# Adjacency columns shared by groups of four edge tiles with half-precision cells, and a reordered set-up

## The reference, cut to what matters

```python
# layer 0
m = silu(einsum('ei,ej,ijh->eh', x[dst], edge_attr_8, W_msg_tp) / sqrt(128))
agg = segment_sum(m @ W_msg_lin / 4, src)
# layer 1, six times, with different W
h = x @ W
agg = segment_sum(h[src] * norm[:, None], dst)      # norm = dinv[src] * dinv[dst]
h = leaky(agg + h * dinv**2 + b)
```

## Time and profile before

| | us |
|---|---|
| median of 3 runs (11523.59 to 11538.84) | 11527.22 |
| profiled execution, its time | 11525.68 |
| its span, first to last instruction | 11523.9 |
| PE busy in the span | 8973.8 |
| DVE busy | 7298.7 |
| POOL busy | 6700.9 |
| ACT busy | 4035.9 |

### The profile page before, as it was taken

The page is one execution under the profiler, slowest core; times in us unless marked ns, Lnnn a source line. Parts: engine busy times, 40 slices in busy tenths (PEclk is TensorE's granted clock), DMA queues, the critical chain, the costliest instruction groups (busy, mean ns, idle before and its releaser), DMA issues.

```text
span 11523.9 us, 201355 instructions
## 1 busy us (share of the span) xinstructions
PE 8973.8 (78%) x51270; PEld 6020.0 (52%) x51270; DVE 7298.7 (63%) x14361; ACT 4035.9 (35%) x11725; POOL 6700.9 (58%) x6789
## 2 busy tenths in 40 slices
PE   0499999998488998857666666688888868888886
PEld 0266666663367777742222222455555645555554
DVE  1498999995122222227777777677777767777776
ACT  2445333332000010005555555344444434444443
POOL 0588788777100000007777777577777757777775
PEclk9999999996588888855555555555555555555555
DMA  6733443440887877882222222111111111111111
GB/s 240 249 98 101 119 109 108 108 109 5 290 282 250 269 245 247 296 279 37 39 38 38 38 38 38 25 20 20 20 20 20 20 21 20 20 20 20 20 20 20
DMA packets 1340632, 1146.59 MB, mean 99 GB/s; under 512 B 329039, under 2 KB 1225504, under 8 KB 1340190
## 3 DMA queue, kind: packets, MB, share of 16 engines
q1 hardware_dynamic: 1108690, 1064.47, 29.1%
q0 software_dynamic: 210560, 44.35, 5.2%
q10 hardware_dynamic: 21186, 34.95, 1.2%
HBM read 994.01 MB, written 144.62 MB: 99 GB/s over the span
## 4 chain that ended last, share of the span: by engine, by line
POOL 31%; PE 14%; issue 12%; DMA 8%; DVE 7%; DVEq 1%; ACT 1%; SPq 1%; POOLq 0%; ACTq 0%
POOL arena L569 31%; PE ps L820 8%; DMA arena<-adj 5%; DVE msg L1779 3%; PE ps L754 2%; DVE arena L1774 2%; DMA arena<-tab,idx 2%; PE ps L935 2%; DVE acc L1266 1%; PE ps L797 1%; PE ps L633 1%; ACT x_all L1106 0%; SPq L455 0%; DMA arena<-rT 0%; DVE x_all L1606 0%
## 5 line engine op out<-in xcount | busy, mean ns | idle before, releaser
L569 POOL DMA_INDIRECT arena<-tab,idx x4896 | 4675.6, 955 | 3843.8 <-DMA idx<-in_src_p 2290.4
L935 PE MATMUL ps<-w_w2b,arena 33*128 33x256 f32 x6528 | 2928.1, 639 | 603.1 <-DMA arena<-rT 594.9
L935 PEld LDWEIGHTS ps<-w_w2b,arena 33*128 33x128 f32 x6528 | 2103.8, 330 | 1223.1 <-issue 686.9
L598 POOL DMA_INDIRECT adj<-pairs x1632 | 1868.7, 1145 | 491.4 <-issue 420.8
L1266 DVE TENSOR_TENSOR acc<-acc,ps 48x128 f32 x4920 | 1377.7, 280 | 660.0 <-DVE acc L1266 12.6
L820 PE MATMUL ps<-arena 128*128 128x192 bf16 (+1 forms) x18816 | 1341.5, 234 | 229.9 <-DMA arena<-adj 214.4
L820 PEld LDWEIGHTS ps<-arena 128*128 128x128 bf16 x18816 | 1282.7, 103 | 303.0 <-issue 293.7
L1774 DVE TENSOR_TENSOR arena<-ps,arena 128x512 f32<-128x512 f32 x1632 | 1012.8, 682 | 190.2 <-DMA arena<-tab,idx 186.6
L633 PEld LDWEIGHTS ps<-arena,threes 128*48 128x48 bf16 x4912 | 486.9, 152 | 1232.9 <-issue 1232.9
L633 PE MATMUL ps<-arena,threes 128*48 128x128 bf16 x4912 | 628.1, 309 | 642.5 <-DVE threes L1275 638.1
L1013 ACT ACTIVATE wide<-ps,not_all 128x128 bf16<-128x128 f32 x1632 | 572.8, 377 | 1241.3 <-PE ps L701 1241.1
(11 more groups left out here) (250 smaller groups left out, 10654.0 us busy)
## 6 DMA issues: line engine op xcount, KB each, us to landing
arena<-adj SPq DMA_DIRECT2D x672, 896.0 KB, 7.3
arena<-rels SPq DMA_DIRECT2D x204, 512.0 KB
arena<-tab SPq DMA_DIRECT2D x1632, 64.0 KB
adj<-zero SPq DMA_DIRECT2D x49, 2048.0 KB, 20.8
arena<-tab,idx POOLq DMA_INDIRECT x4896, 2.4
arena<-rT SPq DMA_DIRECT2D x408, 128.0 KB
adj<-pairs POOLq DMA_INDIRECT x1632
rT<-spare ACTq DMA_DIRECT2D x204, 128.0 KB
```

The lines of the kernel that those rows point to most:

```text
L569: pool.indirect_dma_start(G[b][:, u, 0:FEAT[PHASES[p]]], None, TABLE[PHASES[p]], bass.IndirectOffsetOnAxis(ap=idx[b // 2][:, b % 2 * HT + ...
L598: pool.indirect_dma_start(adj_cells, bass.IndirectOffsetOnAxis(ap=pairs[h][:, u, 0:1], axis=0), pairs16[h][:, u, 2:3], None).then_inc(cell ...
L935: last = mm(ps[:, 4 + q, (u % 2) * 256:(u % 2 + 1) * 256], row[h][0:33, u * P:(u + 1) * P], w["w2b"][:, :], start=True, stop=True)
```

## The change

1. **Columns.** Four tiles in sequence (`R` = 4) share their columns: column = dst + number of the group of four. `Q` falls to 6656 (13 groups of 512 instead of 16), while rows of `adj` stay 8192 cells apart (`QROW`). Cells are fp16 instead of bf16. A code is now source x 512 + place in the group, 23 planes. `compare` multiplies the codes of a tile with those of its group of four: eight 128x512 products per batch, each in a bank of its own of two.
2. **Order in stage 0.** PE does the compares of tiles 0 and 1 of batch k+1 ahead of the scatter of batch k and those of tiles 2 to 7 one by one behind its tiles 0 to 5, each behind a wait for ACT's count two tiles before. ACT makes counts 0 to 2 ahead of the SILU, 3 and 4 behind the first cast, 5 to 7 behind the second, all of the same batch. DVE casts the counts last.
3. **Cells.** POOL writes from DVE's array itself, without the copy; it goes through two batches at once, and the four tiles of a group in turn, each behind the landing of the one before. Fully unrolled.
4. **Passes.** 13 groups; the loops of SP, PE and DVE are unrolled.
5. **Set-up.** ACT issues the plane stores (four buffers) and makes the 52 signs between casts and rows. A0 has two buffers and reads `xT` directly. SP issues 41 zeroing DMAs (of 6656 columns) right behind the first loads, and the last 8 after the loads of three batches.

```diff
-FAR = 1 << 20
+FAR = 1 << 22
-Q = 1 << QBITS
+QROW = 1 << QBITS
+R = 4
+TQ = T // R
+Q = -(-(N + TE // R - 1) // QG) * QG
+NG = Q // QG
-BITS = 21
+BITS = 23
...
-            zero_table()
+            zero_table(0, NS - ZEROS_LATE)
             sp.wait_ge(w_in, 16 * LOADED)
-            sp.wait_ge(tbl_out, tables(1))
+            for j in range(2):
+                sp.wait_ge(rows_stored[j], 16 * ((NC + 1 - j) // 2))
             sp.wait_ge(rels_out, 16)
...
-            edge_loads0()
+            edge_loads0(0, range(3))
+            zero_table(NS - ZEROS_LATE, NS)
+            edge_loads0(0, range(3, SL))
+            with sp.Fori(1, IT) as it:
+                edge_loads0(it, range(SL))
...
+            for k in range(0, NB, 2):
+                pool.wait_ge(vec[0].sem, vec[0].at(k + 1, COUNTED))
+                for i in range(R):
+                    for g in range(2 * HT // R):
+                        t = k * HT + g * R + i
+                        if i > 0:
+                            pool.wait_ge(celled[g], 16 * (k // 2 * R + i))
+                        pool.indirect_dma_start(
+                            adj_cells, bass.IndirectOffsetOnAxis(ap=pair[:, t, 0:1], axis=0),
+                            pair16[:, t, 2:3], None).then_inc(celled[g], 16)
...
+            def compare(h, u, steps):
+                g = u // R * R * P
+                mm(ps[:, 6 + u % 2, :], codes[h][:, u * P:(u + 1) * P], codes[h][:, g:g + R * P],
+                   start=True, stop=True).then_inc(ten[0].sem, steps)
...
-                    pe.wait_ge(scl[0].sem, scl[0].at(k - 1, EQ0 + HT - 1))
-                    pe.sem_inc(pe_go, 1)
-                    compare(k + 1, 1 - h)
+                    for u in range(2):
+                        pe.wait_ge(scl[0].sem, scl[0].at(k, EQ[HT - 2 + u]))
+                        pe.sem_inc(pe_go, 1)
+                        compare(1 - h, u, 1)
...
-                    last.then_inc(ten[0].sem, 1)
+                    last.then_inc(ten[0].sem, 2 if last_batch and u + 2 < HT else 1)
+                    if not last_batch and u + 2 < HT:
+                        pe.wait_ge(scl[0].sem, scl[0].at(k + 1, EQ[u]))
+                        pe.sem_inc(pe_go, 1)
+                        compare(1 - h, u + 2, 1)
...
-                with pe.Fori(0, NG // GB) as it:
-                    for g in range(GB):
+                for G in range(NG):
...
             for j in range(BITS):
+                i, turn = j % len(bit16), j // len(bit16)
                 act.wait_ge(bit_made, j + 1)
...
+                if j % 2 == 1:
+                    tile_signs(j // 2, j // 2 + 1)
+                act.wait_ge(bit_cast, j + 1)
+                act.dma_start(bits[j, :].rearrange("(t e) -> t e", e=TR * P), bit16[i]).then_inc(bits_out[i], 16)
+            for c in range(NC):
+                act.wait_ge(rows_made, c + 1)
+                if c >= 2:
+                    act.wait_ge(rows_stored[c % 2], 16 * (c // 2))
+                act_fn(A_ROWS[c % 2], ps[:, c % 2, :], ACT.Copy).then_inc(rows_cast, 1)
+                tile_signs(BITS // 2 + 2 * c, BITS // 2 + 2 * c + 2)
...
             def messages(it, b):
                 k, h = it * SL + b, b % 2
+                act.wait_ge(vec[0].sem, vec[0].at(k - 2, COUNTED))
+                count_equals(k, h, (0, 1, 2))
                 act.wait_ge(vec[0].sem, vec[0].at(k, PRED))
...
                 act_fn(threes[h][:, :, 0, :], msg[h][:, :, :], ACT.Copy).then_inc(scl[0].sem, 1)
+                count_equals(k, h, (3, 4))
...
+                count_equals(k, h, (5, 6, 7))
...
-                dve.wait_ge(scl[0].sem, scl[0].at(k - 1, EQ0 + HT - 1))
-                nc.vector.tensor_copy(pair16[:, ds(k * HT, HT), 2], equals[h][:, :]).then_inc(v.sem, 1)
                 dve.wait_ge(v.sem, v.at(k, LOW))
                 place(h, 2)
+                dve.wait_ge(scl[0].sem, scl[0].at(k, EQ[HT - 1]))
+                nc.vector.tensor_copy(pair16[:, ds(k * HT, HT), 2], equals[h][:, :]).then_inc(v.sem, 1)
```

More of the change, by code:

```diff
@@ L363, in nodes_done, with cells_done @@
         def nodes_done(eng, p):
[L365 to L370, removed]
+            for i in range(SETS):
+                eng.wait_ge(wave_sem[i], wave_base(PHASES[p], i) + WAVES[PHASES[p]] * len(range(i, NC, SETS)))
+        def cells_done(eng):
+            for x in celled:
+                eng.wait_ge(x, 16 * T // len(celled))
+        ZEROS_LATE = 8
         CONSTS = GR * (1 + 2 + 8 + 6)
@@ L712, in _ @@
             pe.wait_ge(codes_in[0], 16)
-            compare(0, 0)
-            pe.wait_ge(ten[0].sem, ten[0].at(-1, CODED))
-            pe.sem_inc(ten[0].sem, TPER[0] - 2)
+            for u in range(HT):
+                if u >= 2:
+                    pe.wait_ge(scl[0].sem, scl[0].at(0, EQ[u - 2]))
+                compare(0, u, 1 if u == 0 else 3 if u == HT - 1 else 2)
             def messages(it, b, last_batch):
@@ L825, in sum_pass @@
-                combine(NG - 1, 1)
+                for G in range(NG):
+                    par = G % 2
+                    pe.wait_ge(vec[p].sem, vec[p].at(G - 2, PART))
+                    for bank in range(2):
+                        mm(ps[:, 2 * par + bank, 0:2 * W], zero16[:, 0:P], pieces[:, 0:2 * W], start=True, stop=False)
+                    for j in range(NCH):
+                        if j == 2:
+                            combine(G - 1, 1 - par)
+                        turn, i = slot(p, G, j)
+                        pe.wait_ge(blocks[i], 16 * (turn + 1))
+                        for s in range(SC):
+                            for u in range(GB):
+                                last = mm(ps[:, 2 * par + u // 2, u % 2 * W:(u % 2 + 1) * W],
+                                          ring[i][:, s, u * P:(u + 1) * P],
+                                          rows[:, j * SC + s, :, :].rearrange("p k f -> p (k f)"),
+                                          start=False, stop=(j == NCH - 1 and s == SC - 1 and u % 2 == 1))
+                        last.then_inc(ten[p].sem, 1)
@@ L1348, in _ @@
             tile_rows = lambda x: x[0:T // TR, :].rearrange("p (t e) -> p t e", e=P)
+            group_rows = lambda x: x[0:T // TR, :].rearrange("p (t e) -> p t e", e=R * P)
+            in_group = [arena[:, (8 + half) * HE:(9 + half) * HE] for half in range(2)]
             for half in range(2):
@@ L1414, in _ @@
             v = vec[0]
-            before = node[PHASES[0]]
-            dve.wait_ge(before.sem, before.at(NC - 1, before.per))
             dve.sem_inc(v.sem, (SL - 1) * VPER[0])
```

361 lines of the change are left out of this document (116 added, 245 removed).

## The result

The changed kernel takes **11491.7 us** (median of 8 runs, 11488.8 to 11497.8) where the kernel before, beside it, takes 11525.8: ratio **0.997, interval 0.996 to 0.998**. The forecast was 11432. The sign is right and the time is in the range, but of the 95 us that were forecast only 34 came. A later comparison gave 11492.5 against 11520.1, ratio 0.998 (0.997 to 0.999).

What follows compares the result with a forecast made beforehand. TensorE (PE) was taken to set the pace of stage 0, DVE close behind. Terms -155 + 18 + 261 + 254 - 45 - 49 - 331 - 48 = -95 took 11525.7 to 11431, said as 11432 of the median; range 11170 to 11600.

Steps and rivals of the forecast that it cites:

- Set-up: Before the first expand: zeroing queued right behind the loads brings the first expand to 286 instead of 441.5 us, -155.
- +31: In the set-up: us added to the zeroing for the 23 bit planes that go beside it.
- zeros slower than 345 GB/s: In the set-up: one of three things the prediction said would make it wrong.
- Stall before batch 3: Early stage 0: batch 3's loads stand behind the other 8 zeroing DMAs, +18 us (0 to 30).
- Columns, +261: Stage 0: each of 8 compares streams 512 columns, not 128; 1.28 us per batch over 204 batches, +261 us.
- Changes of shape, +254: Stage 0: steps to or from 21-row weights go from 2 to 14 per batch, 0.104 us each, +254 us.
- Rival 1: Stage 0: the shape steps cost nothing between long matmuls; 11178 us, chance 0.21.
- Early batches and clock, -45: Stage 0, first 69 batches: most of 0.9 us each lost to ACT's signs goes, -45 us (0 to -62).
- Rival 2: Stage 0: the granted clock falls, at 0.9 adding 260 us; 11692 us, chance 0.14.
- POOL's tail, -49: After N0, the first node stage: POOL ends some 20 us after the batches, beside N0, -49 us (0 if it lags).
- Passes, -331 - 48: Six summing passes: 13 groups instead of 16, -331 us; unrolled loops lose their turns, -48 us (+20 to -60).
- rival 3: Passes give less and the set-up waits for ACT; 11517 us, from 11490 to 11560, chance 0.15.

Runs made afterwards that it cites:

- planes_spread: Changed kernel with each bit plane stored by two DMAs, rows 0 to 95 and 96 to 101; 15018 us beside 14499 for the kernel before, ratio 1.036, chip with pauses.
- planes_first: Changed kernel with SP waiting for all bit planes before its first 41 zeroing DMAs; 15044 us beside 14499 for the kernel before, ratio 1.038, chip with pauses.
- late_one_3: Changed kernel with the last 8 zeroing DMAs one behind each of batches 3 to 10's loads; repeat, 15073 us beside 14501, ratio 1.040, chip with pauses.
- three_again: Changed kernel with planes stored over 96 and 6 rows, codes of 128 rows, late zeroing DMAs one per batch; 11127.1 us, ratio 0.966 to the kernel before.
- straight0: Changed kernel with stage 0's four-batch loops written out on SP, PE, DVE and ACT; 11476.1 us beside 11492.5 for the changed kernel, ratio 0.996.
- before_straight: Kernel before with the loops of the six summing passes written out, still 16 groups; 14425 us beside 14499, ratio 0.995, on a chip with pauses.
- rows128: Changed kernel with codes widened from 23 to 128 rows, the new ones zeroed; 14596 us beside 14499 for the kernel before, ratio 1.006, chip with pauses.

## Why the prediction was right and wrong

**Set-up: the step that failed.** The forecast took the zeroing at the 344 GB/s of before and added "+31" for the planes, their DMA time (share 0.30 of 94.8 us), as if every engine had an equal part of it. The share was read as a load, and it was a limit: 0.30 to 0.38 of sixteen engines is five or six engines full and ten empty. A zeroing DMA has packets for all sixteen and gets on at the pace of the six. From 60 to 180 us 7252 zero packets of 1664 bytes were sent, 12.1 MB; at the 375 GB/s of later it would have been 45 MB, so 33 MB or 88 us were lost, not 31. That the zeros by themselves are faster than the forecast's rate (371 to 385 GB/s, 182 to 188 us instead of 203) gave some of it back. The price of the mechanism is shown by planes_spread: 48 to 52 us for another division of the rows, which bring the first expand to 287 to 291 us, where the forecast had 286. The prediction named it among what would make it wrong ("zeros slower than 345 GB/s"), but had no row for two DMAs of different width at the same time. The 103 us that the set-up did give come in planes_first too (first expand at 337.7, 104 us sooner than before), so the early place gives none of them. There SP's zeroing takes 188 us instead of 283, the planes end 6 us sooner and the loads behind take 3 less. Of the 32.9 MB that no longer go ahead of the first loads (49 x 2048 KB less 41 x 1664 KB), 19.3 MB are the smaller table, 51 us at 375 GB/s; 13.6 MB, 36 us, are the eight DMAs moved behind the first loads, and most of that is paid again in the stall before batch 3. ACT was misjudged too, without a cost: its signs ended at 276 us, not 245, which the zeroing hid.

**Stall before batch 3.** Forecast +18, at most 30. The distance of 40.9 us between two expands in place of 12.9 is 28; late_one_3 with 12.9 and three_again with 11.5 show that the place of the 8 late zeroing DMAs is its cause.

**Columns, +261.** Right: the step at 128 rows is 1.21 us = 0.996 + 0.21, and 0.21 is 512 columns at 0.417 ns.

**Changes of shape, +254.** Right, and now shown and not only argued: 14 steps give 1.45 us, 0.104 each, or 254 us for the twelve new ones. (The rows gave 0.09 to 0.10 per step; the 0.104 of the sum stands in none of them, so its last digit is luck.) By the Trainium skill, "TensorEngine Tiling (Array Packing)", section Key Properties, a change of tiling mode drains the engine. The trace fits that, as the gap goes with the number of rows while columns, waits and order stay; a drain as such is in no row. Rival 1 (the steps are free between long matmuls) falls. The forecast took this as a price of the change. It was also the largest thing to gain, at no cost in instructions.

**Early batches and clock, -45.** 38 went. Stage 0 grew by 505 us, 204 periods by 204 x (12.92 - 10.40) = 515, the stall added 28, and so what the batches lose beside their period fell by 38, from 73 to 35 us. 18 of these 35 are the wait at batch 12 (30.7 us from expand to expand), which no part of the change touches and which the forecast had spread over 69 batches as if the signs caused all of it; 6 more are turns of the loop (14.0 us instead of 12.9, six times), which straight0 doesn't have. With 10 more for the stall and 7 less here stage 0 misses by 17. The granted clock is 0.99 over stage 0. Rival 2 falls.

**POOL's tail, -49.** 47.3 came.

**Passes, -331 - 48.** The sum of the six distances is 1262.8 us; 1654.1 before. 61 of the 391 belong to the turns of the loop, by before_straight, and 1593.3 - 1262.8 = 330.5 to three groups and fewer waits. The forecast had 48 for the turns of 12 groups, and the rest comes from steadier groups: passes 2 to 5 run at 17.62 us per group almost throughout. The measured 11491.7 lies just outside the forecast's own 11360 to 11490 and just inside the 11490 to 11560 of rival 3 (the passes give less, the set-up waits for ACT), but neither of rival 3's reasons is what happened: unrolling did gain, and the set-up waited for DMA engines, not for ACT, which ended its signs at 276 us, before the zeros were in.

## What to carry to other kernels

Before two transfers are laid over each other, ask how many DMA engines each of them fills, not how busy they are on average: a store of 102 rows filled six of sixteen, and everything that wanted all sixteen went at their pace. Here 96 and 6 rows instead of 102 were enough to fill them. Price a moved transfer by what it takes from its new neighbours, and a postponed one by who will stand behind it. Where short matmuls stand between long ones, try to give them the same number of rows, if need be with zeros: a step in and out of a narrower shape cost 0.2 us here, as much as the 512 columns themselves.

## What the runs showed of the hardware

**102 rows, six engines.** 6 x 17 = 102 and 16 x 6 = 96; a division of the rows into equal parts over at most sixteen engines would give what was seen. That this is the rule was not tried with a third number.

**Chips with pauses.** On four of five chips the kernel before took 14493 to 14760 us instead of 11520. Every variant of the changed kernel with 23-row compares and loops was then 1.036 to 1.044 of it: there the change is a loss (the changed kernel itself wasn't run there; planes_first, equal to it in all stages else, stands for it). The pauses sit at the same places of each loop of four batches, on ACT and PE mostly, and SP at times spends 0.7 us or more on instructions that take 0.03 us elsewhere. ACT and SP in order of time, from rows128 (kernel line numbers are one to three higher there):

```profile
2039.50 0.19 ACT L961 ACTIVATION_READ_ACCUMULATOR wide<-ps,not_all 128x1 f32 x1
2044.67 0.69 ACT L961 ACTIVATE wide<-ps,not_all 128x512 uint8<-128x512 f32 x1 [4.98 <-remote]
```

```profile
2035.87 9.55 SPq L522 DMA_DIRECT2D arena<-tab  x8
```

PE's compare, for which this ACTIVATE waits, had ended at 2040.2; the eight loads of SP take 3.97 us in the undisturbed trace. Straight code in stage 0 took away 43% of the pauses' time. What they are stays open: the number, the bytes and the median duration of the instruction queues' packets are the same on both kinds of chip (65 and 144 packets), so more or slower packets of these queues are not what is seen.

**Two packet sizes.** 1664-byte and 2048-byte packets took 71 and 90 ns in the mean once the planes were out, 23 bytes per ns each; the smaller element of the changed table costs nothing.
